# Twelve layer normalizations in one decoder kernel: one activation table, inputs written tile by tile, the last one in blocks of a batch

## What is computed

```
def _layernorm(x, axis=-1, eps=1e-05):
    m = jnp.mean(x, axis=axis, keepdims=True)
    v = jnp.var(x, axis=axis, keepdims=True)
    return (x - m) / jnp.sqrt(v + eps)
...
x = _layernorm(x + _L0_attn_ref(x, ...), axis=-1)
x = _layernorm(x + _L0_xattn_ref(x, ctx_512, ...), axis=-1)
...
x = _layernorm(x + _L3_ffn_ref(x, ...), axis=-1)
```

## Time and profile before

| what | value |
|---|---|
| median of 3 runs | 3275.51 us |
| the profiled execution | 3273.4 us |
| its span, first to last instruction | 3271.6 us |
| mean granted TensorE clock | 0.946 of full |
| PE busy | 3018.1 us (92%) |
| DVE, ACT, POOL busy | 1438.3, 1070.9, 551.4 us |
| instructions | 37735 |

### The profile page before, as it was taken

One profiled execution on the slowest core, in us unless ns is written; L12 is line 12 of the kernel. 1 busy time (PEld: TensorE's weight loads), 2 busy tenths in 40 slices (PEclk: granted clock), 3 DMA queues, 4 the chain that ended last, 5 costly groups with the idle time before them and its releaser, 6 DMA issues.

```text
span 3271.6 us, 37735 instructions
## 1 busy us (share of the span) xinstructions
PE 3018.1 (92%) x14730; PEld 1914.0 (59%) x14730; DVE 1438.3 (44%) x2735; ACT 1070.9 (33%) x2983; POOL 551.4 (17%) x509
## 2 busy tenths in 40 slices
PE   8899989999889999999898889999999887999978
PEld 4455555555655556667655555555554554677757
DVE  5620276102735446521236665565536666211114
ACT  2210272101623333322145222223313662344431
POOL 0000020000200000024112321120000020577750
PEclk9999989999899999999899999999989988999986
DMA  4011101100011101158400110101100101696556
GB/s 161 22 43 45 65 24 68 47 32 0 13 41 41 52 15 49 44 200 303 137 19 12 36 37 19 37 15 55 39 20 26 49 21 52 214 318 231 181 169 145
DMA packets 66965, 253.32 MB, mean 77 GB/s; under 512 B 25594, under 2 KB 27642, under 8 KB 54852
## 3 DMA queue, kind: packets, MB, share of 16 engines
q1 hardware_dynamic: 32064, 182.08, 16.5%
q0 software_dynamic: 31344, 65.30, 5.9%
q10 hardware_dynamic: 3380, 3.53, 0.4%
HBM read 278.73 MB, written 42.13 MB: 98 GB/s over the span
## 4 chain that ended last, share of the span: by engine, by line
PE 72%; DVE 13%; ACT 7%; DMA 4%; POOL 2%; issue 2%; SPq 0%; POOLq 0%; ACTq 0%; DVEq 0%
PE P L954 32%; PE P L956 13%; PE P L1292 7%; PE P L962 3%; PE P L1186 3%; PE P L1168 3%; ACT A L1420 3%; PE P L1312 2%; DMA A<-tokens,A 1%; DVE A L1853 1%; DVE A L1851 1%; DVE A L1852 1%; PE P L967 1%; ACT A L1471 1%; PE P L964 1%
## 5 line engine op out<-in xcount | busy, mean ns | idle before, releaser
L954 PE MATMUL P<-A,W 128*128 128x400 f32 (+1 forms) x1744 | 622.1, 495 | 12.6 <-DVE A L1881 6.8
L1348 ACT ACTIVATE A<-P 128x400 f32<-128x400 f32 (+6 forms) x589 | 308.5, 531 | 727.6 <-PE P L956 296.3
L954 PEld LDWEIGHTS P<-A,W 128*128 128x128 f32 x1744 | 328.2, 192 | 258.1 <-issue 19.2
L954 PE MATMUL P<-X,W 128*128 128x400 f32 x1008 | 387.7, 523 | 19.9 <-DVE X L1693 11.6
L954 PEld LDWEIGHTS P<-X,W 128*128 128x128 f32 x1008 | 196.4, 199 | 168.2 <-issue 25.8
L2168 POOL TENSOR_TENSOR A<-A,small 100x1600 f32<-100x1600 f32 x32 | 91.6, 2862 | 1144.5 <-DVE small L1733 1144.5
L962 PE MATMUL P<-C,A 128*128 128x128 f32 (+5 forms) x1505 | 218.1, 268 | 47.5 <-POOL A L2168 22.6
L2108 DVE TENSOR_TENSOR A<-P,A 128x128 f32<-128x128 f32 (+1 forms) x141 | 44.9, 318 | 455.5 <-ACT A L1545 455.5
L1420 ACT ACTIVATE A<-A,small 100x100 f32<-100x100 f32 (+1 forms) x640 | 227.4, 365 | 31.8 <-DVE small L1728 31.8
L962 PEld LDWEIGHTS P<-C,A 128*128 128x128 f32 (+5 forms) x1505 | 174.2, 146 | 95.3 <-issue 45.5
L956 PE MATMUL P<-A,W 128*128 128x400 f32 (+1 forms) x528 | 213.9, 487 | 0.0
(11 more groups left out here) (268 smaller groups left out, 4468.7 us busy)
## 6 DMA issues: line engine op xcount, KB each, us to landing
W<-weights SPq DMA_DIRECT2D x60, 1024.0 KB, 4.8
A<-experts SPq DMA_DIRECT2D x16, 1536.0 KB, 7.1
W<-experts SPq DMA_DIRECT2D x28, 768.0 KB, 4.4
W<-weights SPq DMA_DIRECT2D x32, 448.0 KB, 3.3
KT<-experts SPq DMA_DIRECT2D x15, 768.0 KB, 5.8
A<-experts SPq DMA_DIRECT2D x14, 768.0 KB, 5.2
A<-outputs SPq DMA_DIRECT2D x4, 1536.0 KB, 19.9
W<-outputs SPq DMA_DIRECT2D x4, 1536.0 KB, 23.8
```

The costliest lines, as they stand in the source:

```text
L954: self.e.matmul(out, a, b, start=i == 0, stop=False)
L1348: self.e.activation(out, in_, ACT.Copy).then_inc(*self.of(*item))
```

## The change

It asks ACT for the table that holds ln and exp ahead of the scale 0 of sublayers 0, 2, 5 and 11; writes `x` of half 0 in four instructions, one to a tile, with an event of its own for each, on which the chains on `x` wait matmul by matmul; runs the last normalization in eight blocks of 100 tokens between the combines; brings the queries of heads 0 and 1 of a latent attention together ahead of their `made`; changes the counts of `keep_busy` and adds some ahead of the combines; and stores the output in four parts. Left out below is what only passes a slice of tokens in place of h.

```diff
+def part(c, h):
+    return ss(h) if c.n == 11 else hs(h)
...
         def group(g):
             steps = ahead(4 * g)
+            if g == 0:
+                one, two = ahead(0), ahead(1)
+                steps = [one[0], two[0], one[1], two[1]] + one[2:] + two[2:]
             for h in range(4 * g, 4 * g + 4):
-                nxt = ahead(h + 1) if h % 4 < 3 else []
+                nxt = ahead(h + 1) if h % 4 < 3 and h else []
...
-        first, tail = [[("norm_add", c, h), ("norm_centre", c, h), ("norm_scale", c, h)] for h in range(2)]
+        add, centre, scale = (lambda h: ("norm_add", c, h)), (lambda h: ("norm_centre", c, h)), (lambda h: ("norm_scale", c, h))
         yield "halve", c, 0
+        if c.n == 11:
+            for b in range(NB - 2):
+                yield "halve", c, b + 1
+                yield "combine", c, b
+                yield add(b)
+                if b >= 1:
+                    yield centre(b - 1)
+                if b >= 2:
+                    yield scale(b - 2)
+            yield from (centre(5), scale(4), ("combine", c, 6), add(6), ("halve", c, 7), centre(6), scale(5))
+            yield from (("combine", c, 7), add(7), centre(7), scale(6), scale(7))
+            return []
+        behind = {3: [add(0)], 4: [centre(0)], 5: [scale(0)]}
+        tail = [add(1), centre(1), scale(1)]
...
-    def chain(self, out, pairs, *job):
+    def chain(self, out, pairs, *job, tiles=None):
         n = len(pairs)
         for i, (a, b) in enumerate(pairs[:-1]):
+            if tiles:
+                self.wait_ge(self.at("x", *tiles, i) or self.at("x", *tiles))
             self.e.matmul(out, a, b, start=i == 0, stop=False)
         a, b = pairs[-1]
+        if tiles:
+            self.wait_ge(self.at("x", *tiles))
...
     # TensorE.norm_centre
-        if h == 1 and c.n in (4, 5, 7, 10, 11):
+        if h == 1 and c.n in (4, 5, 7, 10):
             self.keep_busy(4)
     # TensorE.norm_scale
-        if (h == 0 and c.n < 11) or c.n in (4, 7, 10):
+        if c.n in (4, 7, 10):
             self.keep_busy(4)
+        elif h == 0 and c.n < 11:
+            self.keep_busy(2)
...
     # TensorE.proj (query alike, with tiles=(c.n - 1, half))
+        tiles = None
         for item in p.needs(h):
-            self.wait_ge(self.at(*item))
+            if item[0] == "x" and item[1] >= 0:
+                tiles = item[1:]
+            else:
+                self.wait_ge(self.at(*item))
...
     # TensorE.combine
+        if b == 0:
+            self.wait_ge(self.at("given", c.n, c.NT - 1))
+            self.keep_busy(18 if c.n == 11 else 6)
+        elif c.n == 11:
+            self.keep_busy(3)
         P = self.take(("turn", "acc", c.n, b), ("z", c.n, b))
...
     # ScalarE.norm_scale
+        if h == 0 and c.n in (0, 2, 5, 11):
+            self.e.preload_act_table_set("natural_log_exp_and_others")
         self.wait_ge(self.at("mean", "var", c.n, h))
...
     # VectorE.norm_scale
-        self.e.tensor_tensor(self.k.x[:, :, hs(h)], c.Z[:, :, hs(h)], bc(c.RS[:, hs(h)], [128, 4, H2]), ALU.mult).then_inc(*self.of("x", c.n, h))
+        if h == 0 and c.n < 11:
+            for k in range(4):
+                i = self.e.tensor_tensor(self.k.x[:, k, t], c.Z[:, k, t], c.RS[:, t], ALU.mult)
+                if k < 3:
+                    i.then_inc(*self.of("x", c.n, h, k))
+        else:
+            i = self.e.tensor_tensor(self.k.x[:, :, t], c.Z[:, :, t], bc(c.RS[:, t], [128, 4, n]), ALU.mult)
+        i.then_inc(*self.of("x", c.n, h))
...
     # SyncE.walk
-        for h in range(2):
-            self.wait_ge(self.at("x", 11, h))
-            e.dma_start(v4(od)[:, :, hs(h)], k.x[:, :, hs(h)]).then_inc(k.semaphore("out_stored"), 16)
-        e.wait_ge(k.semaphore("out_stored"), 32)
+        for first, last in ((0, 4), (4, 6), (6, 7), (7, 8)):
+            t = slice(S * first, S * last)
+            self.wait_ge(self.at("x", 11, last - 1))
+            e.dma_start(v4(od)[:, :, t], k.x[:, :, t]).then_inc(k.semaphore("out_stored"), 16)
+        e.wait_ge(k.semaphore("out_stored"), 64)
```

More of the change, by code:

```diff
@@ L148, in hs, with width @@
     return slice(H2 * h, H2 * h + H2)
+def part(c, h):
+    return ss(h) if c.n == 11 else hs(h)
+def width(c, h):
+    return part(c, h).stop - part(c, h).start
 def ss(b):
@@ L859, in moe @@
             yield "combine", c, b
-            if b in (3, 4, 5):
-                yield first.pop(0)
+            yield from behind.get(b, [])
         return tail
@@ L964, in turns, with mean @@
         self.e.transpose(out, in_, ident).then_inc(*self.of(*job))
-    def mean(self, SQ, h, *job):
-        self.e.matmul(self.ps(*job)[:, 0:H2], self.c["mean"], SQ[:, 0, hs(h)], start=True, stop=True).then_inc(*self.of(*job))
+    def mean(self, SQ, t, *job):
+        self.e.matmul(self.ps(*job)[:, 0:t.stop - t.start], self.c["mean"], SQ[:, 0, t], start=True, stop=True).then_inc(*self.of(*job))
     def rms_sc(self, c, w, h):
@@ L972, in rms_sc @@
         self.wait_ge(self.at("sum", "rms", w, h))
-        self.mean(c.SQ, h, "mean", "rms", w, h)
+        self.mean(c.SQ, hs(h), "mean", "rms", w, h)
     def keep_busy(self, n):
@@ L985, in norm_centre @@
         self.wait_ge(self.at("sum", "mean", c.n, h))
-        self.mean(c.SQ, h, "mean", "mean", c.n, h)
-        if h == 1 and c.n in (4, 5, 7, 10, 11):
+        self.mean(c.SQ, part(c, h), "mean", "mean", c.n, h)
+        if h == 1 and c.n in (4, 5, 7, 10):
             self.keep_busy(4)
@@ L1004, in proj @@
             self.wait_ge(self.k.loaded(self.k.load("L0_attn_", "o", m)))
-        self.chain(P[:, 0:H2], [(p.weights(m, k), p.source(k, h)) for k in range(p.kc)], "proj", p.name, m, h)
+        self.chain(P[:, 0:H2], [(p.weights(m, k), p.source(k, h)) for k in range(p.kc)], "proj", p.name, m, h, tiles=tiles)
         if p.piece and p.last == (m, h):
@@ L1123, in query @@
         P = self.take(("proj", "mq", c.n, h, half), ("mq", c.n, h, half))
-        self.wait_ge(self.at("x", c.n - 1, half))
         self.wait_ge(self.k.loaded(p))
-        self.chain(P[:, 0:H2], [(w(h % 4, k), self.k.x[:, k, hs(half)]) for k in range(4)], "proj", "mq", c.n, h, half)
+        self.chain(P[:, 0:H2], [(w(h % 4, k), self.k.x[:, k, hs(half)]) for k in range(4)], "proj", "mq", c.n, h, half,
+                   tiles=(c.n - 1, half))
         if half and h % 4 == 3:
@@ L1370, in norm_centre @@
         self.wait_ge(self.at("centred", c.n, h))
[L1371 removed]
+        t = part(c, h)
+        self.e.activation(c.SQ[:, :, t], c.Z[:, :, t], ACT.Square).then_inc(*self.of("sq", "norm", c.n, h))
     def norm_scale(self, c, h):
+        if h == 0 and c.n in (0, 2, 5, 11):
+            self.e.preload_act_table_set("natural_log_exp_and_others")
         self.wait_ge(self.at("mean", "var", c.n, h))
         P = self.ps("mean", "var", c.n, h)
[L1376 to L1377 removed]
+        RS = c.RS[:, part(c, h)]
+        self.e.activation(RS, P[:, 0:width(c, h)], ACT.Ln, bias=self.c["eps"][:, 1:2]).then_inc(*self.of("std", "norm", c.n, h))
         self.wait_ge(self.at("std", "norm", c.n, h))
@@ L1673, in norm_add @@
         self.wait_ge(self.z_ready(c, h))
-        self.sums(c.SQ, c.Z, h, "mean", c.n, h)
+        self.sums(c.SQ, c.Z, part(c, h), "mean", c.n, h)
     def z_ready(self, c, h):
```

30 lines of the change are left out of this document (14 added, 16 removed).

## The result

On the chip of the comparison the changed kernel takes **3255.9 us** (median of 8 runs, 3247.2 to 3259.9) against 3274.6 (8 runs, 3267.3 to 3278.3) before: ratio 0.994, interval 0.9924 to 0.9955, so faster by 15 to 25 us. Forecast were 3253.3, between 3239 and 3267. The profiled execution of the changed kernel took 3259.8 us, span 3258.0, mean clock 0.952. It is 3.9 us over its median, where the one before was 2.1 under the median shown there, so the two traces differ by 13.6 us where the medians differ by 18.7.

The account below looks back on a forecast made before the run. PE, busy 92% of the span, was taken as the bound, so only its work or waits count. Boundary, sublayer 5 and sublayer 11 terms sum to 22.2 us: 3273.4 to 3251.2, as a median 3253.3, range 3239 to 3267.

Parts of the forecast that it names:

- the tables: Normalizations: four table loads remain of 24 ahead of ln and 24 ahead of exp; ln to exp 1.30 us shorter a half.
- small boundaries: 0 to 1, 1 to 2, 4 to 5, 9 to 10, 10 to 11: half 1's sum earlier, 0.6 us each, 3.0.
- the end of 11: Sublayer 11: normalization in blocks between combines ends the last product at 3262.9 instead of 3267.1: 4.2 us, bounds 0 and 9.
- 3-4: Boundary of sublayers 3 and 4: `x` of half 1 1.7 us earlier, head 1's query and `pq` already done: gain 5.1.
- 4-5: Boundary of sublayers 4 and 5: half 1's sum comes earlier through DVE's first write: gain 0.6 us.
- the tile writes: Four writes about 0.50 us apart replace one of 1.83: first tile 1.3 us earlier, last 0.2 later.
- rival (c): Compiler puts its loads in anyway; three places lose 2.6 us each, two lose 0.7 each: 3262.5 us, chance 0.06.
- 2-3: Boundary of sublayers 2 and 3: projection starts at 794.3 instead of 796.30, gain 2.0 us, all kept.
- 6-7: Boundary of sublayers 6 and 7: new query order delays the second fold: loss 1.0 us, between gain 1 and loss 4.
- Sublayer 5: Six fillers restore the clock before the combines, so sublayer 6 starts 7.8 us sooner; 2.7 if the clock does not return.
- rival (a): Clock does not follow the fillers; sublayer 5 gives 2.7 us, sublayer 11 nothing: 3262.6 us, chance 0.22.
- Rival (b): Combines of sublayer 11: fillers become a wall at half clock, 13.9 us a block against 7.9 of transfer: 3311.4, chance 0.06.

Follow-up runs that it names:

- experiment 2: Changed kernel without the four requests for the ln and exp table, so 60 loads are back: 3355.8 us, ratio 0.9979 to the kernel before.
- experiment 11: Kernel before the change plus only the four table requests: 3348.9 us, ratio 0.9962.
- experiment 4: Changed kernel without fillers ahead of the combines of sublayers 5 and 11 and without the wait for the last stored result: 3356.1 us, ratio 0.9973.
- experiment 9: Changed kernel with `x` of half 0 written by one instruction again instead of four: 3335.4 us, ratio 0.9921.
- experiment 6: Changed kernel with the old order of the queries in sublayer 7: 3245.4 us, ratio 0.9915.
- experiment 8: Changed kernel with halving 7 ahead of combine 6, no fillers ahead of combines 6 and 7, old query order in sublayer 7, nine fillers in 5: 3245.2 us, ratio 0.991.
- experiment 12: Changed kernel with old query order in sublayer 7, halving 7 ahead of combine 6, one filler ahead of combines 6 and 7: 3331.2 us, ratio 0.9912.
- experiment 1: Changed kernel unaltered, profiled and timed again on another chip: 3336.5 us, ratio 0.9931 to the kernel before.
- the trace after: First profiled execution of the changed kernel, on the chip of the comparison: 3259.8 us.
- experiment 10: Changed kernel with each halving b+1 ahead of combine b in sublayer 11, three fillers kept ahead of combines 6 and 7: 3330.6 us, ratio 0.9894.
- experiment 5: Changed kernel with each halving b+1 ahead of combine b in sublayer 11, no fillers ahead of combines 6 and 7: 3245.7 us, ratio 0.9917.

## Why the prediction was right, and where its terms were off

The time fell as forecast, 18.7 us where 22.2 were given, and by two mechanisms that were named and are shown by leaving them out: the tables (experiments 2 and 11) and the clock under the fillers (experiment 4). But terms were off both ways. The small boundaries gave more than forecast, mostly; the end of 11, 3-4 and 4-5 gave less, and the tile writes nothing. That the sum came out so near is in part luck. One of my own signs of being wrong was seen in the profiled execution, PEclk 0.50 in the combines of 5, and so was another: in five of the seven gaps between the combines of 11 the fillers end after the group has been halved, by 0.6 to 7.8 us.

- **The tables** were under-priced: 9.2 us hung on them in rival (c), and their removal costs 16 to 19 (experiment 2); alone they bring 6 to 19. The step that failed is the one for the five small boundaries, "it waits for the sum of half 1, which comes 0.6 earlier because DVE's first write does", with nothing for them in (c). The sum comes 0.8 earlier (mean 9.29 us after ln of half 0, then 8.47 to 8.50), and that is all the load of half 0, which held up exp, DVE's product and with it the subtraction of half 1: 0.85 with the tables alone, and back at 9.49 without the requests. The stretches gained more than the mean where the clock helped (0-1: 2.3 and 3.9 us). Five times 1.0 and the 9.2 are 14 of the 16 to 19. The rival itself, that the loads stay, is out: four were left. That a load costs 1.28 and no drain more was right.
- **Writes by tiles** were over-priced by reason, not in the sum: 0.50 apart was right (2.02 us for four), but nobody waits for the first tile at 3-4, since two `pq` end later. At 2-3 it does let the projection start 1.0 us sooner, but "all kept" is not borne out: without the tile writes the stretch is not longer (experiment 9).
- **3-4** gained 4.3 of 5.1. All steps happened: no idle of 1.98, one wait of 3.20. Of the missing 0.8, 0.2 is that the query of half 1 starts 1.5 us earlier after ln, not 1.7, and 0.4 that it takes 5.5 us at half clock, 5.0 before. The 0.67 by which the mean of half 1 waits behind the query of head 1 I had not counted; they cost little, as `x` is there 13.0 us after ln and 12.9 were forecast. **2-3** gained 2.4 to 3.5 where I had 2.0; **8-9** between -0.9 and 1.2 (1.1), experiment 2 aside, and the spread is that of the clock; **7-8** 0 to 1.2 (0).
- **4-5** lost 1 to 3 us where 0.6 were forecast as gain. The wait for half 1's sum did shrink, from 3.28 to 2.46 us; but then the clock was low for 10.24 us over the router's small matmuls, not 6.83. With the tables alone it was 6.83 and the stretch 0.8 shorter.
- **6-7**: a loss of 1.0 was forecast, in traces of the new order it is between 0 and 3.9; but the old order has the same spread (experiments 6, 8 and 12: 587.9, 587.7, 585.0). The order is not shown to cost anything.
- **Sublayer 5**: 7.8 if the clock comes back, 2.7 if not. Both were nearly seen: 8.9 in experiment 1, 4.1 in the trace after, where it came and went. With six fillers it held in seven traces of nine. That fillers alone lift it, against rival (a), is shown by experiment 4. The Trainium skill's rule that activity releases the throttle (TensorE: Matmul & The Clock Gate, What's actually happening) fits the fillers, but the combines of experiment 4 ran at 0.50 while busy 18.92 us of 27.31.
- **The end of 11** was over-priced: 4.2, measured 0.8 and 1.0, and even these are the shorter last store, which I had put down as "store as before". The last product was to come 4.2 us sooner; after the last `give` it comes at 95.0 and 95.1 us, 94.8 before. Most combines ran at full clock (4.61 us, 8.85 before), as forecast; combine 2 took 8.2 at half clock. What failed is "three fillers (2.0)" ahead of combine 6: they took 4.25 at half clock, behind idles of 2.74 and 1.28 us. The chain behind combine 7 took 6.1 us and not 4.9. And I had written down that halving 7 stands behind combine 6 without seeing that this order is the price: halving 7 starts without a wait for a transfer, and experiments 10 and 5 have 5 and 10 us back by moving it, with the fillers and without. Rival (b), fillers as a wall for all blocks, did not occur; in the gap ahead of combine 6 it did.

The gathers of 5, 4.3 us longer by chance, explain half of the 8.6 us by which the profiled execution missed 3251.2.

## What to carry to other kernels

A table load costs its whole chain: follow it past the next engine to the last wait that it delays. Here a load of 1.28 us in half 0 held up a mean of half 1 by 1.0 us, two engines on. Matmuls of constants in front of a train of small matmuls pay where they lie in time that waits for a transfer anyway; where they stand between results on the way to the end, they can cost what they take (4.25 us for three, at half clock). Leaving them out there is no sure gain either: the end took 88.0 and 95.4 us without them, as the clock held or fell. In an in-order queue, work whose data have landed goes ahead of the work that waits for another engine.

## What was not expected

- Outside every edit, the same code runs at different clocks: a stretch at 0.50 falls on fillers in one trace and on a query in the next. This moves single stretches by 1 to 7 us, and eight runs of the changed kernel span 13 us, more than most terms of the sum. The differences are not loose ones: from norm 7 to the first gather of 11, eleven traces with the same steps there take 427.3 to 427.4 us (five of them) or 433.2 to 433.3 (six), and nothing between; before the change it was 434.9. So a pair of traces shows a gain of 1.6 or of 7.5 us for the same edit.
- The gathers of sublayer 11 on two chips, first the chip of the result, then that of experiment 1 (columns as in the earlier trace rows), with the longest waits of PE in these stretches:

```profile
2782.00:3159.00 377.00, 368.38 (x2499) 287.33 (x2497) 62.73 (x282) 177.69 (x340) 278.21 (x274) 1.00 0.70 233
```

```profile
PE P L992 <- DMA A<-tokens,A: 4.3, 8, 0.9
```

```profile
2762.30:3231.00 468.70, 384.86 (x2499) 297.53 (x2497) 62.28 (x282) 171.88 (x340) 278.27 (x274) 0.97 0.56 187
```

```profile
PE P L1328 <- ACT A L1389: 73.1, 41, 3.9
```

The same transfers pass at 187 instead of 233 GB/s and PE is idle 84 us instead of 9. The waits are put down to ACT, which is less busy than on the other chip; that it is the loads of experts is a guess, and was not tried. A comparison across chips would have drowned the change in these 90 us; each kernel had the kernel before beside it.
